# Perceiver block: first-stage loads reordered, ternary weights staged in the feed-forward's buffers and rounded between attention pairs

## The reference, cut to what matters

```
q = n(x) Wq ; k = ctx Wk ; v = k Wv ; x += softmax(q k^T / 16) v          # cross attention, stage A
s = 1 / max(mean |w|, 1e-5) ; wq = clip(round(w s), -1, 1) / s            # ternary weights w1, w2
x += w2q(act_quant(silu(conv(w1q(act_quant(n(x)))))))                     # feed-forward, stage F
```

## Time and profile before

| | |
|---|---|
| time, median of 3 runs | 2728.81 us (2725.84 to 2732.73) |
| the profiled execution's own time | 2730.85 us |
| its span | 2729.1 us |
| PE busy | 2525.6 us (93%) |
| DVE busy | 1685.6 us (62%) |
| ACT busy | 1389.3 us (51%) |
| POOL busy | 838.3 us (31%) |
| mean granted TensorE clock | 0.967 |

### The profile page before, as it was taken

How to read it: one execution, slowest core, us unless ns; L and a number is a source line. 1 busy time by engine, 2 the same in 40 slices (tenths; PEclk the granted TensorE clock), 3 DMA queues, 4 the chain that set the end, 5 groups by cost and what they waited for, 6 DMA issues and landing times.

```text
span 2729.1 us, 75620 instructions
## 1 busy us (share of the span) xinstructions
PE 2525.6 (93%) x32404; PEld 2174.9 (80%) x32404; DVE 1685.6 (62%) x3003; ACT 1389.3 (51%) x2233; POOL 838.3 (31%) x857
## 2 busy tenths in 40 slices
PE   6999986789999999999999999999999976999997
PEld 3566655678888888888888888888888855999997
DVE  3467777436566565575665666755756555777775
ACT  1244443445555555555555555555556523555663
POOL 1010012343344434434334344344343300111111
PEclk9999997899999999999999999999999976999999
DMA  9886740560011001100100011011001102666664
GB/s 345 318 315 269 279 181 13 149 207 26 26 42 38 30 30 38 42 30 26 54 26 30 30 38 42 30 34 46 26 30 42 52 1 104 205 202 204 208 202 144
DMA packets 61265, 283.47 MB, mean 104 GB/s; under 512 B 5137, under 2 KB 36242, under 8 KB 46354
## 3 DMA queue, kind: packets, MB, share of 16 engines
q1 hardware_dynamic: 52818, 268.73, 27.6%
q0 software_dynamic: 8160, 10.29, 2.4%
HBM read 247.45 MB, written 33.65 MB: 103 GB/s over the span
## 4 chain that ended last, share of the span: by engine, by line
PE 58%; issue 12%; DVE 11%; DMA 7%; POOL 6%; ACT 5%; SPq 0%; POOLq 0%; DVEq 0%; ACTq 0%
PE PS L1450 7%; PE PS L1286 6%; PE PS L1274 5%; DVE mpart L1816 3%; PE PS L1195 3%; PE PS L1263 3%; PE PS L1261 3%; PE PS L1262 3%; PE PS L1446 3%; DMA unit_raw<-in_experts 3%; POOL ctx_lo L603 2%; PE PS L1170 2%; DMA sum_d<-scaled,xg 2%; PE PS L1252 2%; DVE sideB L1805 2%
## 5 line engine op out<-in xcount | busy, mean ns | idle before, releaser
L1816 DVE TENSOR_REDUCE mpart<-PS 128x1 f32<-128x802 f32 (+1 forms) x512 | 484.7, 986 | 213.7 <-PE PS L1274 212.7
L930 ACT ACTIVATE probs<-PS 128x1024 f32<-128x1024 f32 (+1 forms) x416 | 413.5, 1025 | 219.2 <-PE PS L1450 219.2
L603 POOL TENSOR_TENSOR ctx_lo<-ctx_raw,ctx_hi 128x801 fp32r<-128x801 f32 x128 | 227.8, 1790 | 381.5 <-ACT ctx_hi L865 372.9
L595 POOL TENSOR_TENSOR k_lo<-probs,k_hi 128x400 fp32r<-128x400 f32 (+1 forms) x256 | 250.9, 980 | 276.6 <-ACT k_hi L853 276.5
L1450 PE MATMUL PS<-qbd_hi,k_hi 64*128 64x256 f32 (+1 forms) x1664 | 314.8, 375 | 0.0
L1274 PE MATMUL PS<-k_hi,qbd_hi 128*128 128x512 f32 (+2 forms) x1024 | 266.0, 362 | 22.4 <-DVE mpart L1816 12.6
L852 ACT COPY probs<-PS 128x400 f32<-128x400 f32 (+1 forms) x256 | 126.3, 493 | 246.7 <-PE PS L1254 218.3
L1450 PE MATMUL PS<-qbd_lo,k_hi 64*128 64x256 f32 (+1 forms) x1664 | 235.5, 279 | 2.0 <-issue 2.0
L1261 PE MATMUL PS<-wkv_hi,ctx_hi 128*128 128x256 f32 (+1 forms) x832 | 237.3, 285 | 0.0
L1286 PE MATMUL PS<-probs,vals 128*32 128x64 f32 x13312 | 233.8, 221 | 2.7 <-issue 2.6
L1450 PE MATMUL PS<-qbd_hi,k_lo 64*128 64x256 f32 (+1 forms) x1664 | 235.3, 279 | 0.0
(11 more groups left out here) (320 smaller groups left out, 6261.6 us busy)
## 6 DMA issues: line engine op xcount, KB each, us to landing
unit_raw<-in_experts SPq DMA_DIRECT2D x46, 1536.0 KB, 7.1
ctxN<-in_ctxN SPq DMA_DIRECT2D x16, 3328.0 KB, 11.1
ctxT<-in_ctxT SPq DMA_DIRECT2D x16, 3204.0 KB, 11.5
ctx_raw<-in_ctxT SPq DMA_DIRECT2D x64, 801.0 KB, 4.4
slots_d<-pad_rows SPq DMA_DIRECT2D x18, 1040.0 KB, 12.3
xg<-slots_d SPq DMA_DIRECT2D x23, 260.0 KB, 2.7
x<-in_x SPq DMA_DIRECT2D x1, 2048.0 KB, 9.8
sum_d<-x SPq DMA_DIRECT2D x1, 2048.0 KB, 13.8
```

The source lines that it names most:

```text
L595: g.tensor_tensor(k_lo[:, n, a, c:c + width], k_raw[p % 2][:, 0:width], k_hi[:, n, a, c:c + width].bitcast(F32), ALU.subtract).then_inc(s. ...
L603: g.tensor_tensor(ctx_lo[:, a, cols], ctx_raw[:, cols], ctx_hi[:, a, cols].bitcast(F32), ALU.subtract).then_inc(s.ctx_lo_ready, 1)
L930: act.activation(probs[rows, t % PROBS, :], PS[rows, 1024 * (t % 2):1024 * (t % 2) + 1024], ACT.Exp).then_inc(s.pr_ready, 1)
L1816: v.tensor_reduce(mpart[:, pair, half:half + 1], PS[:, at:at + width], AX, ALU.max).then_inc(s.mx_red, 1)
```

## The change

SP issues the three attention weights, x's tiles 0 and 1, `ctxT` and `ctxN` of pair 0, the three self attention weights and the two convolution weights, x's tiles 2 to 5, w1, and then the pairs' loads (`load_pair`). w2 goes behind pair 2's loads, x's tiles 6 to 15 behind pair 3's, the six remaining weights and the 17 pieces of `w_cp` behind pair 4's. The attention weights are staged in `hidden_f[2]`, w1 in `hidden_f[0]`, w2 in `hidden_f[1]`. PE waits for `first_in` of the three attention weights alone; the second fold product moves behind the first queries, and its copy to `vout` behind ACT's first two copies; a tiny ACT copy is put ahead of the wait for the first product. The ternary weights are summed in the middle of pairs 1 (w1) and 3 (w2), with a one-column partition sum on PE at the end of each (bank 3 instead of bank 2), and the six rounding passes lie in the middle of pairs 2, 3, 4 (w1) and 4, 5, 6 (w2). The diff (left out: the line of semaphore names):

```
@@ -377,17 +377,16 @@
...
-        raw = ctxNf
+        raw = hidden_f[2][:, :, :].rearrange("p t n -> p (t n)")
         wqT_raw, wkT_raw, wv_raw = (raw[:, 512 * n:512 * n + 512].rearrange("p (k n) -> p k n", k=KT) for n in range(3))
-        w1_raw = work[:, 0, 0:KT * HID]
-        w2_raw = work[:, 1, 0:HT * D]
-        first_loads = [
-            (wqT_raw, io["w_xqT"]), (wkT_raw, io["w_xkT"]), (wv_raw, io["w_xv"]),
-            (x[:, :, :], io["x"]), (w1_raw, io["w1T"]), (w2_raw, io["w2T"])]
-        loads = [(w[n][:, :, :], io["w_" + n]) for n in WEIGHTS] + [
-            (wo[:, :, :], io["w_o"]), (convw[:, :, :], io["conv_w"]), (convb[:, :], io["conv_b"])]
-        FIRST_IN = 16 * len(first_loads)
-        WEIGHTS_IN = 16 * len(loads)
+        w1_raw, w2_raw = (hidden_f[n][:, :, :].rearrange("p t n -> p (t n)") for n in range(2))
+        fold_loads = [(wqT_raw, io["w_xqT"]), (wkT_raw, io["w_xkT"]), (wv_raw, io["w_xv"])]
+        a_loads = [(w[n][:, :, :], io["w_" + n]) for n in A_WEIGHTS] + [(convw[:, :, :], io["conv_w"]), (convb[:, :], io["conv_b"])]
+        b_loads = [(w[n][:, :, :], io["w_" + n]) for n in WEIGHTS if n not in A_WEIGHTS] + [(wo[:, :, :], io["w_o"])]
+        X_FIRST, X_MORE = 2, 6
+        FIRST_IN = 16 * len(fold_loads)
+        A_WEIGHTS_IN = 16 * len(a_loads)
+        B_WEIGHTS_IN = 16 * len(b_loads)
         XDONE_A = 2 * TILES
@@ -395,30 +394,44 @@
...
         def _(sp):
-            for dst, src in first_loads:
+            for dst, src in fold_loads:
                 sp.dma_start(dst, src).then_inc(s.first_in, 16)
+            sp.dma_start(x[:, 0:X_FIRST, :], io["x"][:, 0:X_FIRST, :]).then_inc(s.x_first, 16)
+            nkeys = ctxN[:, :, :, :].rearrange("p b t n -> p b (t n)")
...
+            def load_pair(i):
+                sp.wait_ge(s.scores_ps, i)
+                sp.dma_start(ctxT[:, :, :], pair_of(io["ctxT"], i)).then_inc(s.ctxT_in, 16)
+                sp.wait_ge(s.av_ps, i)
+                sp.dma_start(nkeys, pair_of(io["ctxN"], i)).then_inc(s.ctxN_in, 16)
             sp.dma_start(ctxT[:, :, :], pair_of(io["ctxT"], 0)).then_inc(s.ctxT_in, 16)
-            for dst, src in loads:
+            sp.dma_start(nkeys, pair_of(io["ctxN"], 0)).then_inc(s.ctxN_in, 16)
+            for dst, src in a_loads:
                 sp.dma_start(dst, src).then_inc(s.weights_in, 16)
-            sp.wait_ge(s.fold_ps, 2)
-            nkeys = ctxN[:, :, :, :].rearrange("p b t n -> p b (t n)")
-            sp.dma_start(nkeys, pair_of(io["ctxN"], 0)).then_inc(s.ctxN_in, 16)
+            sp.dma_start(x[:, X_FIRST:X_MORE, :], io["x"][:, X_FIRST:X_MORE, :]).then_inc(s.x_more, 16)
+            sp.dma_start(w1_raw, io["w1T"]).then_inc(s.w1_in, 16)
+            load_pair(1)
+            load_pair(2)
+            sp.dma_start(w2_raw, io["w2T"]).then_inc(s.w2_in, 16)
+            load_pair(3)
+            sp.dma_start(x[:, X_MORE:TILES, :], io["x"][:, X_MORE:TILES, :]).then_inc(s.x_rest, 16)
+            load_pair(4)
+            for dst, src in b_loads:
+                sp.dma_start(dst, src).then_inc(s.b_weights_in, 16)
             sp.wait_ge(s.cp_zero, 6)
...
             sp.dma_start(w_cp4[HD:HD + 1, 0, :], io["b_p"][0:1, :]).then_inc(s.cp_in, 16)
-            with sp.Fori(1, TILES) as i:
-                sp.wait_ge(s.scores_ps, i)
-                sp.dma_start(ctxT[:, :, :], pair_of(io["ctxT"], i)).then_inc(s.ctxT_in, 16)
-                sp.wait_ge(s.av_ps, i)
-                sp.dma_start(nkeys, pair_of(io["ctxN"], i)).then_inc(s.ctxN_in, 16)
+            with sp.Fori(5, TILES) as i:
+                load_pair(i)
@@ -745,11 +758,9 @@
...
             act.wait_ge(s.consts_ready, NCONST)
+            act.copy(reload[:, :], eps[:, :])
             act.wait_ge(s.fold_ps, 1)
             act.copy(fold[:, :, :].rearrange("p k n -> p (k n)"), bank(0)).then_inc(s.fold_ready, 1)
-            act.wait_ge(s.fold_ps, 2)
-            act.copy(vout[:, :, :].rearrange("p k n -> p (k n)"), bank(1)).then_inc(s.fold_ready, 1)
@@ -836,6 +847,8 @@
...
             copy_qkT()
+            act.wait_ge(s.fold_ps, 2)
+            act.copy(vout[:, :, :].rearrange("p k n -> p (k n)"), bank(1)).then_inc(s.fold_ready, 1)
             for i in range(TILES):
@@ -1055,11 +1068,7 @@
...
             mm.then_inc(s.fold_ps, 1)
-            for o in range(KT):
-                for k in range(KT):
-                    mm = pe.matmul(bank(1, D, at=o * D), wkT_raw[:, k, o * P:o * P + P], wv_raw[:, k, :], start=k == 0, stop=k == KT - 1)
-            mm.then_inc(s.fold_ps, 1)
-            pe.wait_ge(s.fold_ready, 2)
+            pe.wait_ge(s.fold_ready, 1)
@@ -1136,6 +1145,8 @@
...
                     pe.wait_ge(s.xf_ready, TPC * (f + 1))
+                    if f == 0:
+                        pe.wait_ge(s.tern_read, 2)
                     if f >= 2:
@@ -1208,6 +1219,8 @@
...
                 ffn(2 * i + 1)
+                if first:
+                    pe.wait_ge(s.fold_ready, 2)
                 pe.wait_ge(s.attT_ready, T["attT"].up())
@@ -1217,11 +1230,21 @@
...
+            for o in range(KT):
+                for k in range(KT):
+                    mm = pe.matmul(bank(1, D, at=o * D), wkT_raw[:, k, o * P:o * P + P], wv_raw[:, k, :], start=k == 0, stop=k == KT - 1)
+            mm.then_inc(s.fold_ps, 1)
+            pe_pair_a(0)
+            pe.wait_ge(s.weights_in, A_WEIGHTS_IN)
+            pe_pair_a(1)
             pe.wait_ge(s.tern_sum, 1)
-            pe.matmul(bank(2, 2), ones[:, :], small[:, 86:88], start=True, stop=True).then_inc(s.tern_ps, 1)
-            pe_pair_a(0)
-            pe.wait_ge(s.weights_in, WEIGHTS_IN)
-            for i in range(1, TILES):
+            pe.matmul(bank(3, 1), ones[:, :], small[:, 86:87], start=True, stop=True).then_inc(s.tern_ps, 1)
+            pe_pair_a(2)
+            pe_pair_a(3)
+            pe.wait_ge(s.tern_sum, 2)
+            pe.wait_ge(s.tern_read, 1)
+            pe.matmul(bank(3, 1), ones[:, :], small[:, 87:88], start=True, stop=True).then_inc(s.tern_ps, 1)
+            for i in range(4, TILES):
                 pe_pair_a(i)
@@ -1233,6 +1256,7 @@
...
+            pe.wait_ge(s.b_weights_in, B_WEIGHTS_IN)
             count = [0]
@@ -1594,26 +1618,34 @@
...
-            v.wait_ge(s.first_in, FIRST_IN)
+            v.wait_ge(s.x_first, 16)
             v.wait_ge(s.consts_ready, NCONST)
             layer_norm(x[:, 0, :]).then_inc(s.xn_ready, 1)
-            for n, r in enumerate((w1_raw, w2_raw)):
-                v.tensor_reduce(small[:, 86 + n:87 + n], r, AX, ALU.add, apply_absolute_value=True).then_inc(s.vec_step, 1)
-            v.wait_ge(s.vec_step, T["step"].up(2))
-            v.tensor_copy(carrier_v[:, :], eps[:, :]).then_inc(s.tern_sum, 1)
-            v.wait_ge(s.tern_ps, 1)
-            v.tensor_scalar(small[:, 80:82], bank(2, 2), 1.0 / (HID * D), 1e-5, ALU.mult, ALU.max).then_inc(s.vec_step, 1)
-            v.wait_ge(s.vec_step, own())
-            v.reciprocal(small[:, 82:84], small[:, 80:82]).then_inc(s.vec_step, 1)
-            v.tensor_scalar(small[:, 84:86], small[:, 80:82], 1 / 127, None, ALU.mult).then_inc(s.vec_step, 1)
-            v.wait_ge(s.vec_step, T["step"].up(2))
-            for n, (r, q) in enumerate(((w1_raw, w1q), (w2_raw, w2q))):
-                v.tensor_scalar(r, r, small[:, 82 + n:83 + n], MAGIC, ALU.mult, ALU.add).then_inc(s.vec_step, 1)
+            tern = ((w1_raw, w1q), (w2_raw, w2q))
+            def tern_sum(n):
+                v.wait_ge((s.w1_in, s.w2_in)[n], 16)
+                v.tensor_reduce(small[:, 86 + n:87 + n], tern[n][0], AX, ALU.add, apply_absolute_value=True).then_inc(s.vec_step, 1)
                 v.wait_ge(s.vec_step, own())
-                v.tensor_scalar(r, r, MAGIC, 1.0, ALU.subtract, ALU.min).then_inc(s.vec_step, 1)
-                v.wait_ge(s.vec_step, own())
-                v.tensor_scalar(q[:, :, :].rearrange("p a n -> p (a n)"), r, -1.0, None, ALU.max).then_inc(s.vec_step, 1)
+                v.tensor_copy(carrier_v[:, :], eps[:, :]).then_inc(s.tern_sum, 1)
+            def tern_scale(n):
+                mean, inv, step = (small[:, 80 + 2 * k + n:81 + 2 * k + n] for k in range(3))
+                v.wait_ge(s.tern_ps, n + 1)
+                v.tensor_scalar(mean, bank(3, 1), 1.0 / (HID * D), 1e-5, ALU.mult, ALU.max).then_inc(s.tern_read, 1)
+                v.wait_ge(s.tern_read, n + 1)
+                v.reciprocal(inv, mean).then_inc(s.vec_step, 1)
+                v.tensor_scalar(step, mean, 1 / 127, None, ALU.mult).then_inc(s.vec_step, 1)
+                v.wait_ge(s.vec_step, T["step"].up(2))
+            def tern_round(n, part):
+                r, q = tern[n]
+                if part == 0:
+                    v.tensor_scalar(r, r, small[:, 82 + n:83 + n], MAGIC, ALU.mult, ALU.add).then_inc(s.vec_step, 1)
+                if part == 1:
+                    v.tensor_scalar(r, r, MAGIC, 1.0, ALU.subtract, ALU.min).then_inc(s.vec_step, 1)
+                if part == 2:
```

(21 more changed lines are left out.)

## The result

The changed kernel takes 2717.95 us (median of 7 runs, 2711.14 to 2720.84), the one before 2731.57 in the same comparison (7 runs): ratio 0.995, 95% interval 0.994 to 0.996. In a second comparison it was 2718.35 against 2732.49, ratio 0.9942 (0.9928 to 0.9955). The profiled execution took 2720.84 us, its span is 2719.0 against 2729.1, so 10.1 us between the two profiles. A ratio here is the comparison's own estimate over all its runs and can lie some 0.001 off the quotient of the two medians.

The account below looks back on a forecast made before the run. Stage A was taken as bound by PE's work after a late start, held by the wait for w2. Gains 10.3 + 2.2 - 0.5 = 12.0 us, from the median 2728.81, gave 2716.8 us, range 2711.5 to 2723.0.

Parts of the forecast that it names:

- Start of the first scores: Pair 0's scores on PE start with their context at 15.5 us instead of 25.83: 10.3 us gained.
- PE's head: PE's work before pair 0's scores, started at 5.6 us, is ready at 13.1, 2.4 us before the context.
- Maxima: Pair 0's row maxima on DVE directly follow the scores once the ternary passes leave the head: 2.2 us gained.
- DVE: Ternary work fits DVE's waits before the self attention's add in pairs 3, 4 and 6, pair 6 with 0.9 us spare.
- One-column sums: Two matmuls on PE, now standing between pairs, cost at most 0.28 us each: 0.5 us lost.
- Pair 1's transfer: Pair 1's ctxT lands at 36.0 us, wanted at 38.0; no stall taken, 1.2 us at the upper end.
- Pair 5's transfer: Pair 5's ctxT, issued at 108.2 us, lands by 120 to 123, wanted at 122.7; no stall taken.
- The slower rival: SP held at small loads ahead of pair 5, its ctxT 15.6 to 22.8 us late: 2732.4 to 2739.6; chance 0.07.
- Clock: Low clock before pair 0's transposes may stay away, a gain of 1.4 to 1.7 us; nothing taken.
- The rival of the low clock at the first scores: PE, working with gaps before 15.5 us, meets the scores at the lower clock: 1.9 us, 2718.7; chance 0.07.
- Slower delivery: Queue moves as little as 319 GB/s, pair 1's ctxT lands at 42.7, stall 4.7 us: 2721.5; chance 0.05.
- shared landing: Pair 0's ctxT and ctxN share the engines and land together at 23.5 us; 4.0 us gained, 2724.8; chance 0.06.

Follow-up runs that it names:

- extra_pass: Changed kernel plus one more value-neutral DVE pass over 128x2048 values in the middle of each of pairs 1 to 6; 2715.71 us, ratio 0.9932.
- tern_only: Changed kernel with the old order of the loads and the old wait for all six first loads; 2729.17 us, ratio 0.998.
- x_whole: Changed kernel with x loaded whole (2048 KB) ahead of pair 0's ctxT instead of its first 256 KB; 2724.64 us, ratio 0.996.
- pe_filled: Changed kernel plus 14 matmuls nobody reads on PE between pair 0's scores and its transposes; 2724.86 us, ratio 0.997.
- b_early: Changed kernel with the six later weights and w_cp's 17 pieces loaded ahead of pair 1's loads; 2724.83 us, ratio 0.9972.
- fold_late: Changed kernel with the second fold product behind pair 0's scores and its copy behind the exponential; 2719.83 us, ratio 0.9955.
- lean_head: fold_late with w_xv and x's second tile (384 KB) loaded behind pair 0's ctxT; 2720.94 us, ratio 0.9957.
- split_first: lean_head with pair 0's ctxT loaded in two pieces, scores starting with the first; 2714.93 us, ratio 0.9946.
- split_deep: split_first with pair 1's ctxT ahead of x's tiles 2 to 5 and w1 behind pair 1's ctxN; 2712.97 us, ratio 0.9949.
- pe_filled_7: Changed kernel plus 7 matmuls nobody reads on PE between pair 0's scores and its transposes; 2714.64 us, ratio 0.9948.

## Why the prediction was right

**Start of the first scores.** Forecast 15.5, measured 15.6 and 16.1. The context, forecast from the bytes ahead at 424 GB/s, landed at 15.4 and 14.8 (and at up to 16.1, in extra_pass, with the same loads in the same order). The start is right, and tern_only shows that the gain is the order's. What sets it is only half right: in the first profile landing and head met (15.4 and 15.5), in the second the head ended 1.3 us behind the landing. For 1792 KB more x_whole had the landing 4.9 and 5.5 us later, where the price per byte has 4.3.

**PE's head.** Here the working failed: "ready at 13.1", a cover of 2.4 us. The head took 9.7 us from its start in the changed kernel, not 7.5, and ended at 15.5. Two things are in the 2.2 us. First, the second product had run from 20.61 to 22.5 in the old head, beside the table load (20.89 to 22.17); taking the load out and leaving the product under it counted that time twice. Second, the clock. The old head's queries took 1.16 us, the changed kernel's 2.08, and the transposes 0.70 instead of 0.44. Before:

```profile
20.61 1.91 PE L1060 MATMUL PS<-ctxN 128*128 128x256 f32 x8
...
24.21 1.16 PE L1075 MATMUL PS<-xnT,fold 128*128 128x128 f32 x8 [0.46 <-ACT xnT L745]
```

pe_filled, whose head is the changed kernel's:

```profile
11.98 1.16 PE L1084 MATMUL PS<-xnT,fold 128*128 128x128 f32 x8 [0.46 <-ACT xnT L758]
12.98 1.89 PE L1239 MATMUL PS<-hidden_f 128*128 128x256 f32 x8
```

With the clock up, as here and in b_early, the same head takes 8.2 us, so 0.7 us are the product's and 1.5 the clock's. It isn't the product's new place alone that keeps the clock down: with the product behind the queries or later they took 2.1 us in eight of twelve profiles, 1.16 in three and 1.34 in one, and what decides it the runs don't show. The sum stayed right because the head, even so, ended no more than 0.6 us behind the 15.5 forecast for the landing. That is luck: there was no cover left under which the move "costs nothing".

**Maxima.** 2.2 forecast; they follow the scores at once. Right.

**DVE.** Everything fits, measured 1.67, 2.13 and 1.77 us left in pairs 3, 4 and 6. In pair 6 I had 0.9: DVE had waited 0.8 there for ACT inside its own work, and a pass ahead of that wait is free. extra_pass, with a second pass in the same place, bears this out.

**One-column sums.** 0.5 lost was the bound. The pairs with one are 0.12 us longer (21.16 for pair 1 to 2, 21.04 before), 0.24 in all.

**Pair 1's transfer.** 36.0 forecast, 36.7 landed, used at 39.2. Right.

**Pair 5's transfer.** Issue forecast 1.5 us behind the scores, measured 3.2 (111.31 against 108.1): w_cp's pieces took 8.5 us for 16, not 7.4. The six weights took 3.1 us, not 2.6. It landed at 123.8, past the "120 to 123", since the pairs themselves ran 1.4 us behind the forecast; against their own start it is inside, 0.4 us before use. The slower rival was the right place to look, but ahead of pair 5 no weight held SP over 0.52 us. The long holds stand at the head, where SP has nothing else to do (2.81 us at x's tiles 2 to 5, 3.31 at w1), and in b_early.

**Clock.** "The low level may stay away" was left at nothing in the sum, and it came in both profiles of the changed kernel; in one it cost 1.1 us more than before. I had bounded this only as a gain; a lower bound below nothing was missing. That is what makes stage A's gain 11.0 in the profiled execution instead of 12.0; in the second profile it is 11.9. It is also most of why pair 5's scores came at 124.2, not at the 122.7 given as a sign; in the second profile they came at 123.2. The rival of the low clock at the first scores had against it that the clock stood "gaps of 1.2 us" in the old head. That gap is the weight loads'; PE's own longest was 0.8. It didn't come true in the changed kernel, but did in five with other heads or other idle time before the scores: b_early 7.30, fold_late 7.33, lean_head 7.86, split_first 8.57 and split_deep 6.79 us instead of 5.60, so 1.2 to 3.0 us more, around the forecast's 1.9. The Trainium skill, TensorE: Matmul & The Clock Gate, What's actually happening, has the low rate as the default that activity releases. The traces agree: in every profile the first product, with PE idle before it, takes 3.4 to 3.8 us, and one of the same size behind pair 0's scores 1.99.

**Queue rivals.** Slower delivery and shared landing are out: pair 0's `ctxT` landed at 15.4 and its `ctxN`, issued right behind it, at 23.6 (3.17 + 20.4), 8.2 us later, 416 GB/s. The Trainium skill's figure of 358 GB/s (DMA: Bandwidth & Descriptors, Specifications) isn't a limit here: from 8 to 20 us the changed kernel's profile has 427 to 439 GB/s in each window of 2 us. The same page's Bandwidth section has 425 GB/s for 16 MB issued from GpSimd with the other core of the pair idle, and the trace is near that; that was the figure of the page to weigh in the prediction.

**The rest of the time.** Stage A explains 11.0 to 11.9 of the 13.6 and 14.1 us. The other 2.6 and 2.2 us aren't explained. Stage B began 12.2 us earlier in the changed kernel's profile and ended 8.7 us earlier, in its second profile 12.8 and 14.1. "Shifted by 12 us and otherwise as before" thus held for its start only, and that the time came out within 1.2 us of 2716.8 is in part luck.

## What to carry to other kernels

Order the first loads by first use, add up the bytes ahead of the one that the bound engine waits for, and compare with that engine's own work up to there: past the point where they meet, a change to one alone brings little. Here splitting the context and shortening the queue behind it brought the most in stage A (4.6 to 5.5 us), and none of it showed in the ratio of the times. Work taken out of the front of a TensorE-bound kernel leaves idle time, and the matmuls after it may run at the low clock, which took back most or all of what an earlier start had won in fold_late, lean_head and split_first. Work moved into a long wait of PE can keep the clock up behind it (pe_filled_7, fold_late), but only as much as the wait holds (pe_filled), and not each time (split_first). Passes put into an engine's waits are free for as long as the row before its next wait for the bound engine shows more than their length.

## What the runs showed of the hardware that I had not expected

- Scores of the same shape took 5.6 us in some kernels and 6.8 to 8.6 in others. With the second product ahead and 1.0 us idle (pe_filled) they took 5.60; without it and 1.1 us idle (fold_late) 7.33; with it and 2.0 us idle (b_early) 7.30. Each is one profile, and the clock's level in the head differed between profiles of the same code too (queries 1.16 or 2.08 us), so how much of it is the edit's isn't shown.
- A wait of 3.8 us before pair 0's transposes was enough for the clock to fall in each of the six profiles that had it unfilled (transposes 2.84 to 3.04 us), and 3.3 us of matmuls without readers in it cost nothing and won 1.4 to 2.9 us. With 1.9 us of it left the transposes took 1.64 us in three profiles and 2.66 in split_first.
- The changed kernel's stage B took 1700.2 us in one profile and 1695.4 in the other, with a granted clock of 0.87 and 0.97 from 540 to 600 us. Over all thirteen profiles that clock and stage B's length don't go together.
- SP needs 0.46 to 0.53 us for each 16 KB piece, and in b_early their issue, behind holds of 3.95 and 2.97 us at two weights with the queue full, had the next context issued 7.2 us behind pair 0's scores (29.8 against 22.6).
